# Attention outputs of a fused cross-attention and expert kernel: P V in plain fp32 on two column tiles, softmax sums off TensorE, V kept on chip

## The chip, the cores and the metric

The kernel runs on one core of a Trainium2 chip. The metric is the device time of one execution in microseconds (us). The kernel before was run three times: 1199.52, 1198.44 and 1197.42 us, median 1198.44 us.

## The reference, cut to what matters

```python
# x 2048 x 256, ctx 1601 x 192; 4 heads of 64; keys = 1601 ctx rows (masked) and 2048 latent rows
q = ln @ Wq.T
kv = concatenate([xn @ Wkv.T, ln @ Wlkv.T], axis=1)          # ctx keys, then latent keys
...
qn, kn = rmsnorm(q, qn_g) * SCALE, rmsnorm(k, kn_g)
attn = softmax(where(mask, einsum('bhid,bhjd->bhij', qn, kn), -max), axis=-1)
out = einsum('bhij,bhjd->bhid', attn, v)                     # P V, the part that changes
x = x + out @ Wo.T + bo
...
x = x + top-2 mixture of 8 experts of layernorm(x)           # silu(gate) * up, 256 -> 512 -> 256
```

All arithmetic is fp32, and the kernel keeps close to that precision.

## The kernel before, in words

**Prologue.** The keys make 29 tiles of 128 (NK = 29: 13 of context, 16 of latents). A software pipeline (`pro`, written once for each engine, at lines 440, 575, 757 and 1112) normalises a tile, transposes it, multiplies it by the projection weights in plain fp32 (lines 1129 and 1133), normalises K by head, transposes K, and keeps K on chip as two arrays: S2 with the rounded value (type fp32r), the mask and a row for the maximum; S1 with rounded value and remainder one above the other. V is written to DRAM: ScalarE rounds it (line 593), VectorE forms the remainder (line 786), and SyncE stores both with a column of ones (`v_store`, line 285).

**Attention loop.** A unit is one head and 512 queries, 16 units in all. `v_load` (line 292) brings the V of a head back in two buffers. In a unit the 29 key tiles go in 15 pairs (NP = 15; the last pair has one tile). For a pair p the engines do this:

- TensorE, `scores(p)` (line 1214): for each of the two tiles two fp32r products of 512 columns (lines 1221 and 1222) into one of two score banks bS.
- ScalarE (line 642): the exponential of the pair, 128 x 1024, into PT, which has three slots; then (line 648) the rounded copy Ph.
- VectorE or GpSimd (lines 894 and 482): the remainder Pl = PT - Ph. GpSimd takes six pairs of a unit, VectorE nine.
- TensorE, `outputs(p)` (line 1230), issued two pairs behind the scores: for each tile V rounded times Ph (line 1239, 65 output rows, the 65th being the sum of P by the column of ones), V remainder times Ph (line 1241, 64 output rows) and V rounded times Pl (line 1249), all into the bank bPV.

In between, TensorE computes the row maxima of the next unit in 32 `pieces` of 464 columns (line 1177), in two banks bM; VectorE reduces each (line 867). PE can start piece k only when piece k - 2 was reduced. At the start of a unit the next queries are transposed (`q_T`, line 1162), and ScalarE copies them out in `q_evac` and `q_evac_1` (lines 626 and 629) behind the exponentials of pairs 1 and 2; VectorE forms their remainder (`q_lo`, line 861). At pair 4 the outputs of the unit before are transposed back (`o_T`, line 1191; four transposes at line 1200) and divided by the sums (`o_out`, line 880). At the end the maxima are transposed (`c_T`, line 1180) and put into the queries as a row (line 633), which the next unit's scores wait for; ScalarE copies bPV out (line 652).

Each engine runs its own program in the order written, and waits on semaphores. What sets the order around the change is the list `SLOTS` with the pieces' places, and `POOL_PAIRS`. SyncE and GpSimd meanwhile split the expert weights in 96 chunks (`split`, line 462; `store`, line 323), six in a unit.

**Behind the loop** come the output projection, router and 39 expert blocks, which the change leaves as they are.

Of the kernel before, what the change touches and what calls it, by code (L numbers as in the profile page):

```python
# [17 lines left out]
F32 = mybir.dt.float32  # L18
# [19 lines left out]
VW = 2 * D + 1  # L38
NP = (NK + 1) // 2
NG = -(-KEYS // 512)  # L40
# [49 lines left out]
def build(nc, x, ctx_in, mask, ln_x_g, ln_x_b, ln_l_g, ln_l_b, qn_g, kn_g, w_lat, w_ctx, wo_t, bo,  # L90
          router_t, w13, w2, out):
    xln_d = nc.dram_tensor("xln_d", [TOK, DIM], F32, kind="Internal").ap()
    v_d = nc.dram_tensor("v_d", [H, P, NK, VW], F32, kind="Internal").ap()
# [10 lines left out]
    with stack:  # L104
# [25 lines left out]
        Ph = sb("Ph", [P, 3, 2, QB * P], F32R, at=pro)  # L130
# [13 lines left out]
        top = ExitStack()  # L144

# [9 lines left out]
        st6 = sb("st6", [P, NK, 6], at=t0)  # L155
# [7 lines left out]
        Vs = sb("Vs", [P, 2, H, VW], F32R, at=t0)  # L163
        t0.close()
        t1 = ExitStack()
        V = sb("V", [P, 2, NK, VW], F32R, at=t1)
        Q1 = sb("Q1", [P, 2, QB * P], F32R, at=t1)
        Q2 = sb("Q2", [P, 2, QB * P], F32R, at=t1)
        part = ExitStack()
        PT = sb("PT", [P, 3, 2, QB * P], at=part)  # L170
        part.close()
        Pl = sb("Pl", [P, 3, 2, QB * P], F32R, at=t1)
# [3 lines left out]
        oT_a = sb("oT_a", [P, QB * P], at=t1)  # L176
# [97 lines left out]
        def _(sp):  # L274
# [9 lines left out]

            def v_store(s):
                sp.wait_ge(sem("v_lo"), s.v + 1)
                sp.dma_start(v_d[:, :, s.v, :].rearrange("h p c -> p h c"), Vs[:, s.par, :, :].bitcast(F32))\
                    .then_inc(sem(f"v_st{s.par}"), 16)

            run_steps(sp, 0, NK, v_store)  # L290

            def v_load(h):
                sp.dma_start(V[:, h % 2, :, :].bitcast(F32), v_d[h]).then_inc(sem(f"v_in{h % 2}"), 16)

            for j in range(2):
                sp.wait_ge(sem(f"v_st{j}"), (NK + 1 - j) // 2 * 16)
            sp.wait_ge(sem("klo"), NK)
            sp.wait_ge(sem("s1"), NK)
            sp.wait_ge(sem("q_s"), NT)
            v_load(0)  # L300
            v_load(1)
# [37 lines left out]
            for h in range(H):  # L339
                if h < H - 1:  # L340
                    with sp.Fori(0, EH) as i:
                        expert_split(EH * h + i, False)
                else:
                    for e in range(EH * h, E):
                        expert_split(e, e == E - 1)
                if h + 2 < H:
                    sp.wait_ge(sem("pv"), 3 + NP * NB * (h + 1))
                    v_load(h + 2)
# [65 lines left out]
        def _(pool):  # L414
# [11 lines left out]
            pool.memset(Vs[:, :, :, D:D + 1].bitcast(F32), 1.0).then_inc(sem("v1"), 1)  # L426
# [7 lines left out]
            pool.wait_ge(sem("v1"), 1)  # L434
# [38 lines left out]

            NG_ = len(POOL_PAIRS)
            SHARE = NCH * E // UNITS
            for h in range(H):
                with pool.Fori(0, NB // 2) as i:
                    for j in range(2):
                        u = NB * h + 2 * i + j
                        for n, p in enumerate(POOL_PAIRS):  # L480
                            pool.wait_ge(sem("p_hi"), NP * u + p + 1)
                            pool.tensor_tensor(Pl[:, p % 3, :, :], PT[:, p % 3, :, :],  # L482
                                               Ph[:, p % 3, :, :].bitcast(F32), ALU.subtract)\
                                .then_inc(sem("p_lo_g"), 1)
                            for ch in range(SHARE * n // NG_, SHARE * (n + 1) // NG_):
                                split(E // H * h + i, SHARE * j + ch)

# [67 lines left out]
        def _(act):  # L555
# [19 lines left out]
            def pro(s, b, c):  # L575
# [13 lines left out]
                if b:  # L589
                    act.wait_ge(sem("v_mm"), t.v + 1)  # L590
                    if not (t.i is None and t.off < 2):
                        act.wait_ge(sem(f"v_st{t.par}"), 16 * t.half)
                    act.copy(Vs[:, t.par, :, 0:D], heads(bV[t.par][:, 0, 0:DIM])).then_inc(sem("v_hi"), 1)
# [15 lines left out]
            act.wait_ge(sem("v1"), 1)  # L609
# [24 lines left out]

            def unit(u, j):
                for p in range(NP):
# [4 lines left out]
                    act.wait_ge(sem("pv"), g + 1)  # L641
                    act.activation(PT[:, p % 3, 0:w, :], bS[sl][:, 0:w, :], ACT.Exp).then_inc(sem("exp"), 1)  # L642
# [7 lines left out]
                act.wait_ge(sem("pv"), NP * (u + 1) + 3)  # L650
                act.wait_ge(sem("oT_a"), u + 1)
                act.copy(oT_a[0:D + 1, :], bPV[0:D + 1, 0, :]).then_inc(sem("o_cp"), 1)
# [65 lines left out]
        def _(dve):  # L718
# [38 lines left out]
            def pro(s, a, ln, b, c):  # L757
# [61 lines left out]
            dve.wait_ge(sem("v1"), 1)  # L819
# [69 lines left out]
            def p_lo(u, p):  # L889
                w = 2 if 2 * p + 1 < NK else 1  # L890
                if p in POOL_PAIRS:
                    return
                dve.wait_ge(sem("p_hi"), NP * u + p + 1)
                dve.tensor_tensor(Pl[:, p % 3, 0:w, :], PT[:, p % 3, 0:w, :],  # L894
                                  Ph[:, p % 3, 0:w, :].bitcast(F32), ALU.subtract).then_inc(sem("p_lo"), 1)

            def unit(u, j, last):

                q_stage(u + 1, (u + 1) % UNITS if last else u + 1)
                for p in range(NP):  # L900
                    pieces(u + 1, (p, 0))
                    if p:
                        p_lo(u, p - 1)
                    if p == 2:
                        q_lo(u + 1, (j + 1) % 2)
                    if p == 4:
                        o_out(u)
                    pieces(u + 1, (p, 1))
                    pieces(u + 1, (p, 2))
                    if p == SLOTS[-1][0]:  # L910
                        maxima(u + 1)
                p_lo(u, NP - 1)
# [196 lines left out]
        def _(pe):  # L1109
            pe.wait_ge(sem("ident"), 1)  # L1110

            def pro(s, c, a, b):
# [47 lines left out]
            pe.sem_inc(sem("pv"), 3)  # L1160
# [284 lines left out]
```

## Time and profile before

| | |
|---|---|
| median of three runs | 1198.44 us |
| lowest, highest | 1197.42, 1199.52 us |
| profiled execution | span 1197.7 us from the first to the last instruction |
| prologue | 0 to 139 us |
| first maxima, then 16 units | 139 to 860 us |
| projection, router, experts | 860 to 1198 us |
| mean granted TensorE clock | 0.946 |

The profiled execution has no time recorded for it but its span, which lies between the lowest and the highest run. In the profile PE is TensorE's matmul side, PEld its weight loads (which run beside matmuls), DVE VectorE, ACT ScalarE, POOL GpSimd, SPq and the like the queues of DMA issues. A row of the view in order of time has the start, the duration, the engine, the line, the operation, out<-in and the shapes; an entry in brackets is the idle time before it and who ended it. Matmuls overlap in their tails, so that the distance from one start to the next is what one costs, not its duration. "128*65" is the stationary operand: 128 rows, 65 columns. A fp32r product of 512 columns is one record; a plain fp32 product is two records.

### The profile page before, as it was taken

How to read it: one execution, taken by the hardware profiler on the slowest of the kernel's cores; microseconds unless marked ns; L12 is line 12 of the kernel's file. 1: busy time of each engine (PE TensorE's matmuls, PEld its weight loads, DVE VectorE, ACT ScalarE, POOL GpSimd, SP SyncE). 2: the span in 40 equal slices, each digit the busy share in tenths (PEclk: the TensorE clock that was granted, in tenths of full speed). 3: DMA queues.
4: the chain of work that ended last, by engine and by line, in shares of the span. 5: the costliest groups of instructions: out<-in, count | busy, mean ns of one | idle time of the engine just before them, and what ended most of it. 6: DMA issues, size and time to landing. Idle time of an engine off the chain costs nothing.

```text
span 1197.7 us, 19749 instructions
## 1 busy us (share of the span) xinstructions
PE 1054.0 (88%) x4904; PEld 761.3 (64%) x4905; DVE 774.5 (65%) x1474; ACT 656.9 (55%) x867; POOL 518.0 (43%) x525
## 2 busy tenths in 40 slices
PE   3688689999999999999999999999866268999994
PEld 2455457667666666766666766666555257888884
DVE  4999777766766866766766676686554813444442
ACT  1455446777777777777677677777522012333321
POOL 4012125454544654644645554465410014555553
PEclk9899879999999999999999999999977569999998
DMA  5222402112131111231211211111266777333332
GB/s 162 62 71 71 172 16 69 53 40 70 53 113 58 60 46 53 66 114 45 71 48 48 70 53 49 57 58 47 67 184 209 265 248 199 52 49 52 53 53 26
DMA packets 84392, 100.41 MB, mean 84 GB/s; under 512 B 11035, under 2 KB 78044, under 8 KB 83836
## 3 DMA queue, kind: packets, MB, share of 16 engines
q1 hardware_dynamic: 73694, 89.20, 22.8%
q0 software_dynamic: 7488, 10.23, 5.3%
q10 hardware_dynamic: 3166, 0.46, 0.3%
q8 instruction: 19, 0.31, 0.1%
q14 instruction: 25, 0.20, 0.1%
HBM read 57.60 MB, written 42.26 MB: 83 GB/s over the span
## 4 chain that ended last, share of the span: by engine, by line
PE 70%; DVE 10%; ACT 7%; DMA 5%; issue 5%; SPq 1%; ACTq 1%; DVEq 0%; POOL 0%; POOLq 0%
PE bM L1177 9%; PE bPV L1241 8%; PE bPV L1239 8%; PE bPV L1249 8%; PE bS L1221 7%; PE bS L1222 7%; ACT PT L642 4%; DVE mpart L867 3%; DMA xin<-x 3%; PE bA L1129 2%; PE bG L1340 2%; PE bH L1357 1%; ACT Ph L648 1%; PE bY L1340 1%; PE bY L1342 1%
## 5 line engine op out<-in xcount | busy, mean ns | idle before, releaser
L482 POOL TENSOR_TENSOR Pl<-PT,Ph 128x1024 fp32r<-128x1024 f32 x96 | 230.8, 2404 | 348.5 <-ACT Ph L648 348.5
L867 DVE TENSOR_REDUCE mpart<-bM 128x1 f32<-128x464 f32 x524 | 310.9, 635 | 87.2 <-PE bM L1177 85.9
L642 ACT ACTIVATE PT<-bS 128x1024 f32<-128x1024 f32 (+1 forms) x240 | 239.4, 998 | 139.3 <-PE bS L1222 139.3
L648 ACT CAST Ph<-PT 128x1024 fp32r<-128x1024 f32 (+1 forms) x240 | 245.5, 1023 | 7.0
L894 DVE TENSOR_TENSOR Pl<-PT,Ph 128x1024 fp32r<-128x1024 f32 x144 | 176.1, 1223 | 104.6 <-ACT Ph L648 104.4
L1221 PE MATMUL bS<-Q,S 128*128 128x512 f32 x464 | 185.9, 401 | 1.4 <-ACT Q L633 0.7
L1239 PE MATMUL bPV<-Ph,V 128*65 128x512 f32 x464 | 184.5, 398 | 0.0
L1222 PE MATMUL bS<-Q,S 128*128 128x512 f32 x464 | 184.0, 396 | 0.0
L1241 PE MATMUL bPV<-Ph,V 128*64 128x512 f32 x464 | 183.1, 395 | 0.0
L1177 PE MATMUL bM<-S,Q 128*128 128x464 f32 (+1 forms) x524 | 165.5, 390 | 10.9 <-DVE mpart L867 8.7
L1249 PE MATMUL bPV<-Pl,V 128*65 128x512 f32 x464 | 146.9, 395 | 0.8
L1177 PEld LDWEIGHTS bM<-S,Q 128*128 128x128 f32 x524 | 99.3, 190 | 59.7 <-DVE mpart L867 15.6
L1221 PEld LDWEIGHTS bS<-Q,S 128*128 128x128 f32 x464 | 87.8, 189 | 28.7 <-ACT PT L642 3.7
L1222 PEld LDWEIGHTS bS<-Q,S 128*128 128x128 f32 x464 | 87.9, 189 | 17.7
L470 POOL TENSOR_TENSOR wraw<-wraw,whi 128x256 fp32r<-128x256 f32 x96 | 85.8, 894 | 7.7
L1249 PEld LDWEIGHTS bPV<-Pl,V 128*65 128x65 f32 x464 | 61.7, 135 | 42.5 <-DVE Pl L894 8.2
L1241 PEld LDWEIGHTS bPV<-Ph,V 128*64 128x64 f32 x464 | 62.5, 135 | 38.0
L1239 PEld LDWEIGHTS bPV<-Ph,V 128*65 128x65 f32 x464 | 62.9, 136 | 34.9 <-issue 5.8
L538 POOL DMA_INDIRECT out<-ysb,ring_s x39 | 62.2, 1594 | 41.7 <-POOL ring_s L532 32.3
L1090 DVE TENSOR_TENSOR hs<-hs,bU 128x512 f32<-128x512 f32 x39 | 26.8, 687 | 64.2 <-PE bU L1342 64.2
L710 ACT CAST xTe<-bXe 128x256 fp32r<-128x256 f32 x39 | 14.6, 373 | 88.0 <-PE bXe L1378 88.0
L698 ACT CAST hTe<-bH 128x512 fp32r<-128x512 f32 x39 | 22.9, 587 | 67.8 <-PE bH L1357 67.8
(210 smaller groups left out, 1537.4 us busy)
## 6 DMA issues: line engine op xcount, KB each, us to landing
W<-wsp_d SPq DMA_DIRECT2D x32, 768.0 KB, 5.8
wraw<-w SPq DMA_DIRECT2D x96, 128.0 KB, 2.2
wsp_d<-whi SPq DMA_DIRECT2D x96, 128.0 KB, 1.7
wsp_d<-wraw SPq DMA_DIRECT2D x96, 128.0 KB, 1.7
v_d<-Vs SPq DMA_DIRECT2D x29, 258.0 KB, 3.3
V<-v_d SPq DMA_DIRECT2D x4, 1870.5 KB, 7.6
xall<-x SPq DMA_DIRECT2D x1, 2048.0 KB, 13.6
xin<-x SPq DMA_DIRECT2D x16, 128.0 KB, 3.8
```

What stands on the lines that cost most here:

```text
L470: pool.tensor_tensor(wraw[:, ch % 2, :].bitcast(F32R), wraw[:, ch % 2, :], whi[:, ch % 2, :].bitcast(F32), ALU.subtract).then_inc(sem("wsp ...
L482: pool.tensor_tensor(Pl[:, p % 3, :, :], PT[:, p % 3, :, :], Ph[:, p % 3, :, :].bitcast(F32), ALU.subtract)\
L642: act.activation(PT[:, p % 3, 0:w, :], bS[sl][:, 0:w, :], ACT.Exp).then_inc(sem("exp"), 1)
L648: act.copy(Ph[:, p % 3, 0:w, :], PT[:, p % 3, 0:w, :]).then_inc(sem("p_hi"), 1)
L867: dve.tensor_reduce(mpart[:, i, g:g + 1], banks[k % len(banks)][:, 0:PIECE], AX, ALU.max)\
L894: dve.tensor_tensor(Pl[:, p % 3, 0:w, :], PT[:, p % 3, 0:w, :], Ph[:, p % 3, 0:w, :].bitcast(F32), ALU.subtract).then_inc(sem("p_lo"), 1)
L1177: pe.matmul(banks[k % len(banks)][:, 0:PIECE], Q2[:, par, i * P:(i + 1) * P], S2[:, h, g * PIECE:(g + 1) * PIECE], start=True, stop=True). ...
L1221: pe.matmul(bS[sl][:, b, :], S1[:, h, c * P:(c + 1) * P], Q1[:, j, :], start=True, stop=False)
L1222: last = pe.matmul(bS[sl][:, b, :], S2[:, h, c * P:(c + 1) * P], Q2[:, j, :], start=False, stop=True)
L1239: pe.matmul(bPV[0:D + 1, 0, :], V[:, h % 2, c, 0:D + 1], Ph[:, sl, b, :], start=c == 0, stop=False, skip_group_check=True)
L1241: pe.matmul(bPV[0:D, 0, :], V[:, h % 2, c, D + 1:VW], Ph[:, sl, b, :], start=False, stop=False, skip_group_check=True)
L1249: last = pe.matmul(bPV[0:D + 1, 0, :], V[:, h % 2, c, 0:D + 1], Pl[:, sl, b, :], start=False, stop=c == NK - 1, skip_group_check=True)
```

## The change

V stays in SBUF in fp32 (`V[P, H, NK * D]`); its rounding, remainder, stores and loads go. P is no longer split: PT has four slots and is used in plain fp32. The two tiles of a pair go to two column tiles of the array: tile b of the pair writes output rows 64 b to 64 b + 63 of bPV. The sums of P over the keys leave TensorE: VectorE and GpSimd add up PT in two accumulators (`DVE_SUMS`, `POOL_SUMS`), VectorE merges them at the start of the next unit (`z_merge`), and `o_T` becomes eight plain fp32 products a unit: four that add the two halves by a stacked identity (`twin`) while they transpose, and four with a column of ones (`onec`) that add the sums over the partitions. The pieces are placed by `PIECES`, before and behind the outputs of a pair; they begin at pair 2.

```diff
-        Ph = sb("Ph", [P, 3, 2, QB * P], F32R, at=pro)
+        acc_d = sb("acc_d", [P, 2, QB * P], at=pro)
+        acc_p = sb("acc_p", [P, 2, QB * P], at=pro)
...
-                    act.copy(Vs[:, t.par, :, 0:D], heads(bV[t.par][:, 0, 0:DIM])).then_inc(sem("v_hi"), 1)
+                    act.copy(V[:, :, bass.ds(t.v * D, D)], heads(bV[t.par][:, 0, 0:DIM])).then_inc(sem("v_cp"), 1)
...
-                    dve.wait_ge(sem("v_hi"), t.v + 1)
-                    dve.tensor_tensor(Vs[:, t.par, :, D + 1:VW], heads(bV[t.par][:, 0, 0:DIM]),
-                                      Vs[:, t.par, :, 0:D].bitcast(F32), ALU.subtract).then_inc(sem("v_lo"), 1)
...
+            dve.memset(acc_d[:], 1.0).then_inc(sem("z_d"), len(DVE_SUMS))
+            dve.memset(acc_p[:], 1.0).then_inc(sem("z_p"), len(POOL_SUMS))
...
+            def pt_free(u, p):
+                old = p - NPT if p >= NPT else max(q for q in range(NP) if q % NPT == p)
+                since = 1 if p >= NPT else 0
+                act.wait_ge(sem("pv"), NP * (u + since) + old + 1)
+                for name, sums in (("z_p", POOL_SUMS), ("z_d", DVE_SUMS)):
+                    for n, pair in enumerate(sums):
+                        if old in pair:
+                            act.wait_ge(sem(name), len(sums) * (u + since) + n + 1)
...
-                    act.wait_ge(sem("exp"), g + 3)
-                    act.copy(Ph[:, p % 3, 0:w, :], PT[:, p % 3, 0:w, :]).then_inc(sem("p_hi"), 1)
...
+            def z_merge(v):
+                dve.wait_ge(sem("z_d"), ND * (v + 1))
+                dve.wait_ge(sem("z_p"), len(POOL_SUMS) * (v + 1))
+                dve.tensor_tensor(acc_d[:], acc_d[:], acc_p[:], ALU.add).then_inc(sem("zm"), 1)
+                dve.wait_ge(sem("zm"), v + 1)
+                dve.tensor_tensor(zs[:], acc_d[:, 0, :], acc_d[:, 1, :], ALU.add).then_inc(sem("zs"), 1)
...
             def unit(u, j, last):
                 q_stage(u + 1, (u + 1) % UNITS if last else u + 1)
+                z_merge(u)
+                q_lo(u + 1, (j + 1) % 2)
+                done = 0
+                for k, (before, after) in enumerate(PIECES):
+                    n = sum(sum(x) for x in PIECES[:k])
+                    for m in range(before + after):
+                        piece(u + 1, n + m, M_BANKS)
+                    if n < NM <= n + before + after:
+                        maxima(u + 1)
+                    if k == OUT_AT:
+                        o_out(u)
+                    while done < ND and max(DVE_SUMS[done]) < k:
+                        z_sum(u, done)
+                        done += 1
...
+                pe.wait_ge(sem("zs"), v + 1)
...
-                    last = pe.transpose(bT[:, 0, i * (D + 1):(i + 1) * (D + 1)], oT_a[0:D + 1, i * P:(i + 1) * P],
-                                        ident[0:D + 1, 0:D + 1])
+                    at = i * (D + 1)
+                    pe.matmul(bT[:, 0, at:at + D], oT_a[:, i * P:(i + 1) * P], twin[:], start=True, stop=True)
+                    last = pe.matmul(bT[:, 0, at + D:at + D + 1], zs[:, i * P:(i + 1) * P], onec[:],
+                                     start=True, stop=True)
...
                 def outputs(p):
+                    pe.wait_ge(sem("exp"), NP * u + p + 3)
+                    for b, c in enumerate(range(2 * p, min(2 * p + 2, NK))):
+                        last = pe.matmul(bPV[b * D:(b + 1) * D, 0, :], V[:, h, c * D:(c + 1) * D],
+                                         PT[:, p % NPT, b, :], start=c < 2, stop=c >= NK - 2, skip_group_check=True)
                     last.then_inc(sem("pv"), 1)
...
                 for p in range(NP):
                     scores(p)
                     if p == 0:
                         q_T(u + 1)
-                    pieces((p, 0))
-                    if p == 4:
+                    if p == OUT_AT:
                         o_T(u)
+                    pieces(p, 0)
                     if p >= 2:
                         outputs(p - 2)
-                    pieces((p, 2))
+                    pieces(p, 1)
...
+PIECES = ((0, 0),) * 2 + ((2, 1),) * 8 + ((2, 0),) * 4 + ((0, 0),)
+OUT_AT = 4
+POOL_SUMS = ((0, 1), (-1, 3), (-1, 5), (-1, 6), (-1, 8), (-1, 9), (-1, 11))
+DVE_SUMS = ((2, 4), (-1, 7), (-1, 10), (-1, 12), (-1, 13), (-1, 14))
```

GpSimd's `z_sum` has the form of VectorE's: it waits for the exponential of its pair, adds a slot of PT to acc_p, and its first sum of a unit also waits for the merge. Between its sums it does its six splits, as before.

## Rows read from the trace of the kernel before

**Rows 1.** The page: busy time of the engines over the whole span

```profile
PE 1054.0 (88%) x4904; PEld 761.3 (64%) x4905; DVE 774.5 (65%) x1474; ACT 656.9 (55%) x867; POOL 518.0 (43%) x525
```

**Rows 2.** A stretch of the loop: length; PE, PEld, DVE, ACT, POOL; clock, DMA share, GB/s

```profile
195.00:500.00 305.00, 299.34 (x1327) 204.69 (x1326) 216.76 (x324) 226.53 (x240) 159.49 (x126) 1.00 0.18 61
```

**Rows 3.** Line 652, the copy that ends each unit (min/median/max ns, first, last start)

```profile
L652 ACT COPY oT_a<-bPV x16: 581/582/583, 208.6 to 859.4; 65x512 f32<-65x512 f32 x16
```

**Rows 4.** Groups by line, 144 to 880 us: busy, mean ns, idle before, releaser

```profile
L867 DVE TENSOR_REDUCE mpart<-bM 128x1 f32<-128x464 f32 x524 | 310.9, 635 | 87.2 <-PE bM L1177 85.9
...
L482 POOL TENSOR_TENSOR Pl<-PT,Ph 128x1024 fp32r<-128x1024 f32 x96 | 230.8, 2404 | 348.5 <-ACT Ph L648 348.5
L642 ACT ACTIVATE PT<-bS 128x1024 f32<-128x1024 f32 x224 | 229.9, 1026 | 136.8 <-PE bS L1222 136.8
...
L894 DVE TENSOR_TENSOR Pl<-PT,Ph 128x1024 fp32r<-128x1024 f32 x128 | 160.9, 1257 | 101.6 <-ACT Ph L648 101.5
```

**Rows 5.** TensorE in order of time, inside a unit: start us, us, instruction

```profile
500.29 0.39 PE L1221 MATMUL bS<-Q,S 128*128 128x512 f32 x1
500.52 0.39 PE L1222 MATMUL bS<-Q,S 128*128 128x512 f32 x1
500.74 0.59 PE L1177 MATMUL bM<-S,Q 128*128 x2
501.17 0.39 PE L1239 MATMUL bPV<-Ph,V 128*65 128x512 f32 x1
501.40 0.40 PE L1241 MATMUL bPV<-Ph,V 128*64 128x512 f32 x1
501.63 0.39 PE L1239 MATMUL bPV<-Ph,V 128*65 128x512 f32 x1
```

**Rows 6.** The same view, plain fp32 products of the projections

```profile
102.23 1.96 PE L1129 MATMUL bA<-wl,xT 128*128 128x512 f32 x4 [0.50 <-DVE knat L801]
104.02 1.03 PE L1133 MATMUL bV<-wl,xT 128*128 128x256 f32 x4
...
106.20 1.96 PE L1129 MATMUL bA<-wl,xT 128*128 128x512 f32 x4 [0.50 <-DVE knat L801]
```

**Rows 7.** Weight loads of plain fp32 with 128 columns; then the transposes at line 1200

```profile
906.45 0.63 PEld L1311 LDWEIGHTS bL<-rt,x3T 128*128 128x128 f32 x4
906.92 0.28 PEld L1284 LDWEIGHTS bFT<-ident,ost 128*128 128x128 f32 x2
...
523.12 0.41 PE L1200 MATMUL bT<-ident,oT_a 65*128 65x65 f32 x4
523.33 0.42 PE L1239 MATMUL bPV<-Ph,V 128*65 128x512 f32 x1
```

**Rows 8.** The start of a unit in order of time: start us, us, instruction

```profile
512.83 0.40 PE L1221 MATMUL bS<-Q,S 128*128 128x512 f32 x1
...
513.96 1.03 ACT L642 ACTIVATE PT<-bS 128x1024 f32<-128x1024 f32 x1 [0.35 <-PE bS L1222]
...
515.13 0.41 PE L1221 MATMUL bS<-Q,S 128*128 128x512 f32 x1
...
519.36 0.58 ACT L629 CAST Q<-bT 64x512 fp32r<-64x512 f32 x1
...
520.04 0.68 DVE L861 TENSOR_TENSOR Q<-bT,Q 64x512 fp32r<-64x512 f32 x1 [0.37 <-ACT Q L629]
...
521.32 1.03 PE L1177 MATMUL bM<-S,Q 128*128 128x464 f32 x2 [0.52 <-DVE mpart L867]
```

**Rows 9.** The prologue: all V remainders, then VectorE in order of time

```profile
L786 DVE TENSOR_TENSOR Vs<-bV,Vs 128x256 fp32r<-128x256 f32 x29 | 12.3, 424 | 0.8
...
108.36 0.42 DVE L786 TENSOR_TENSOR Vs<-bV,Vs 128x256 fp32r<-128x256 f32 x1
108.70 0.16 DVE L790 TENSOR_SCALAR rn<-nrm 128x8 f32<-128x8 f32 x1
```

**Rows 10.** VectorE between the prologue and the first unit, in order of time

```profile
139.03 0.91 DVE L850 MEMSET Q<- 64x1024 f32 x1 [0.27 <-issue]
```

More of the change, by code:

```diff
@@ L37 @@
 NB = NT // QB
-VW = 2 * D + 1
 NP = (NK + 1) // 2
+NPT = 4
 NG = -(-KEYS // 512)
@@ L282, in _ @@
             sp.dma_start(wl[:], w_lat.rearrange("(k p) n -> p k n", p=P)).then_inc(sem("wl_in"), 16)
[L285 to L296, printed above, removed]
             sp.wait_ge(sem("klo"), NK)
             sp.wait_ge(sem("s1"), NK)
+            sp.wait_ge(sem("v_cp"), NK)
             sp.wait_ge(sem("q_s"), NT)
-            v_load(0)
-            v_load(1)
             NCH = EW // WC
@@ L471, in split, with z_sum @@
                                    whi[:, ch % 2, :].bitcast(F32), ALU.subtract).then_inc(sem("wsplit"), 1)
-            NG_ = len(POOL_PAIRS)
             SHARE = NCH * E // UNITS
+            NZ = len(POOL_SUMS)
+            def z_sum(u, n):
+                p, q = POOL_SUMS[n]
+                if n == 0:
+                    pool.wait_ge(sem("zm"), u + 1)
+                else:
+                    pool.wait_ge(sem("z_p"), NZ * (u + 1) + n)
+                pool.wait_ge(sem("exp"), NP * u + max(p, q) + 3)
+                one = acc_p[:] if p < 0 else PT[:, p % NPT, :, :]
+                pool.tensor_tensor(acc_p[:], one, PT[:, q % NPT, :, :], ALU.add).then_inc(sem("z_p"), 1)
             for h in range(H):
@@ L479, in _ @@
                         u = NB * h + 2 * i + j
[L480 to L485, printed above, removed]
+                        for n in range(NZ):
+                            z_sum(u, n)
+                            for ch in range(SHARE * n // NZ, SHARE * (n + 1) // NZ):
                                 split(E // H * h + i, SHARE * j + ch)
@@ L640, in unit @@
                     act.wait_ge(sem("s_mm"), g + 1)
-                    act.wait_ge(sem("pv"), g + 1)
-                    act.activation(PT[:, p % 3, 0:w, :], bS[sl][:, 0:w, :], ACT.Exp).then_inc(sem("exp"), 1)
+                    pt_free(u, p)
+                    act.activation(PT[:, p % NPT, 0:w, :], bS[sl][:, 0:w, :], ACT.Exp).then_inc(sem("exp"), 1)
                     if p == 1:
@@ new lines, in z_sum @@
+            def z_sum(u, n):
+                p, q = DVE_SUMS[n]
+                w = 2 if 2 * q + 1 < NK else 1
+                if n:
+                    dve.wait_ge(sem("z_d"), ND * (u + 1) + n)
+                dve.wait_ge(sem("exp"), NP * u + max(p, q) + 3)
+                one = acc_d[:, 0:w, :] if p < 0 else PT[:, p % NPT, 0:w, :]
+                dve.tensor_tensor(acc_d[:, 0:w, :], one, PT[:, q % NPT, 0:w, :], ALU.add).then_inc(sem("z_d"), 1)
+            def z_merge(v):
[4 more added lines that the diff above has]
+                dve.tensor_tensor(zs[:], acc_d[:, 0, :], acc_d[:, 1, :], ALU.add).then_inc(sem("zs"), 1)
@@ L914, in _ @@
+                while done < ND:
+                    z_sum(u, done)
+                    done += 1
             dve.wait_ge(sem("q1w"), 1)
@@ L1408 @@
 LAT_AT = 6
-SLOTS = [(p, c) for p in range(3, NP - 1) for c in ((0, 2) if p % 2 else (1,))][:NM // 2]
-POOL_PAIRS = (2, 4, 6, 8, 10, 12)
-DVE_PAIRS = tuple(p for p in range(NP) if p not in POOL_PAIRS)
-assert len(SLOTS) == NM // 2
+PIECES = ((0, 0),) * 2 + ((2, 1),) * 8 + ((2, 0),) * 4 + ((0, 0),)
+OUT_AT = 4
+POOL_SUMS = ((0, 1), (-1, 3), (-1, 5), (-1, 6), (-1, 8), (-1, 9), (-1, 11))
+DVE_SUMS = ((2, 4), (-1, 7), (-1, 10), (-1, 12), (-1, 13), (-1, 14))
+assert sum(sum(x) for x in PIECES) == NM and len(PIECES) == NP
 FFN_SEGMENTS = ((0, 1, (1, 0, 0)), (1, 2, (1, 1, 0)), (2, NBLK, (1, 1, 1)), (NBLK, NBLK + 1, (0, 1, 1)),
```

98 lines of the change are left out of this document (27 added, 71 removed).

## The prediction, made before the changed kernel was run

> **What bounds the kernel now.** I read the busy times first: TensorE is busy for 88% of the span, VectorE for 65%, no other engine for more [rows 1]. Cut by stretches, the attention loop shows TensorE busy for 299 of 305 us at full clock (1.00, the 2.4 GHz level), VectorE for 217, ScalarE for 227 and GpSimd for 159 [rows 2]. The copy that ends each unit starts at 208.6 us in the first and 859.4 us in the last of 16, so a unit takes 650.8 / 15 = 43.4 us [rows 3]. So inside a unit the order and the cost of TensorE's instructions set the time. The groups say the same from the other side: VectorE waits 85.9 us for pieces from TensorE, ScalarE 136.8 us for scores and GpSimd 348.5 us for P, all waiting down the line from TensorE [rows 4].
>
> In order of time a fp32r product of 512 columns costs 0.23 us from start to start (500.29, 500.52; 501.17, 501.40, 501.63) and two pieces 0.43 [rows 5]. A unit's 58 score products make 13.3 us, its 87 output products 20.0, its 32 pieces 6.9, three sets of transposes about 0.9: 41.1 in all, and 2.3 us of waits.
>
> **P V, the main term.** It loses 87 fp32r products and gains 29 plain fp32 products in two column tiles. Plain fp32 costs what the projections show: four records of 512 columns, that is two products, take 104.02 - 102.23 = 1.79 us, or 0.447 a record and 0.895 a product [rows 6]. No row shows two products in different column tiles at once, so I bound it. From below, both tiles stream side by side the whole time: 0.895 a pair. From above, one after the other: 1.79 a pair. Today's six products cost 1.38. I take a value between them for a reason of order: the two records of one product need the same tile and stand next to each other in the program, and in every row matmuls start in program order. If the order holds over tiles too, the first record of tile B can start only when the second of tile A does. Then a pair is A1, then A2 beside B1, then B2: three steps, 1.34 us. The last two outputs of a unit follow each other directly, and B2 of pair 13 runs beside the first record of pair 14: four steps, 1.79. That makes 13 x 1.34 + 1.79 = 19.2 us against 20.0: **-0.8 us a unit**. The two half-used tiles bring nearly nothing, because the pair is too short a run to overlap.
>
> The Trainium skill (TensorE: Matmul & The Clock Gate, Part 3, on what overlaps) says that matmuls are monotone in start and end also over tiles. The rows agree as far as they go, since none starts out of order; by that rule the sum is the one above.
>
> **o_T.** Four transposes cost 523.33 - 523.12 = 0.21 us of TensorE's time now [rows 7]. They become eight plain fp32 products, 16 records, each with a load of 128 stationary columns and with few moving columns. The nearest row is the router's product: four such loads in 906.92 - 906.45 = 0.47 us, 0.118 each [rows 7]. 16 x 0.118 = 1.9: **+1.7 us a unit**, in line with the pieces and outputs behind it.
>
> **The start of a unit.** With scores(0) at 0 (512.83 in the trace), ScalarE's exponential starts at 1.13 and lasts 1.03, and scores(2) starts at 2.30 when it has ended [rows 8]. Now nothing is asked of the next queries until pair 3; the pieces of pair 3 then wait because VectorE's q_lo stands ahead of their reductions (ScalarE's copy at 519.36, q_lo at 520.04, TensorE held to 521.32) [rows 8]. Over this stretch I count 1.6 us of waits on TensorE. After the change the rounded copies of P are gone, so exp(1) ends at 3.45 and the query copy at 4.02; but the pieces now come at pair 2, before outputs(0), and TensorE reaches them at 3.23: it waits 0.9 us. Exp(2) then runs to 5.05, the second query copy to 5.63, q_lo to 6.4, the first reduction (0.6) to 7.0. TensorE's third piece, behind outputs(0), is reached at 5.89 and waits for that bank to 7.1: 1.2 us more. With 0.1 before scores(2) that makes 2.2 us: **+0.6 us a unit**. The waits for Pl that go are counted in this.
>
> **What lies beside other work.** VectorE drops nine remainders (1.26 us each, one of them short, 11 in all) and gains six sums and two merges (nearest row 1.26, halves 0.7, 9.0 in all) [rows 4]: 2 us a unit less. The merge stands ahead of q_lo and the pieces, but it ends near 3 us, before q_lo's inputs exist. A sum between two pairs' pieces makes VectorE 1.26 us late; a pair of TensorE's work is 0.93 + 1.34 + 0.65 = 2.92 and of VectorE's three reductions 1.9, so it catches up within a pair and costs 0.1 or so. ScalarE drops 15 copies of 1 us and stays far from the bound; its new waits for free slots of PT lie after sums that are at least one pair old. GpSimd goes from six additions of 2.4 us to seven [rows 4]: 159.49 us in 305 is 22.7 a unit, so 25.1 of some 45. Its last sum, of pair 11, is three pairs ahead of the merge that waits for it. Behind that merge stand q_lo, all reductions and through them TensorE; this cover of about 7 us would be gone only if GpSimd's splits were held by DMA. SyncE loses the four loads of V from its queue, which were ahead of nobody on the path.
>
> **Once only.** In the prologue VectorE is the busiest engine, and the V remainder stands in its chain: 108.70 - 108.36 = 0.34 us before the next step can start, 29 times [rows 9]: at most -9.9 us; nothing would be the other end, if another engine took over. I take it whole. Before the first unit VectorE gains two memsets of 1024 columns, 0.91 each by the nearest row [rows 10], and three small ones: +2.2. Behind the last unit nothing covers the merge (about +1.2) and o_T (+1.7). Together **-4.8 us**.
>
> **The sum.** 16 x (-0.8 + 1.7 + 0.6) = +24, less 4.8: +19.2 on the span of 1197.7 us, 1216.9. The median of the runs is 0.7 us above that span: 1217.6, and I say 1218.
>
> **Rival 1, full overlap.** B1 starts beside A1. For it: two 64-column tiles share neither columns nor output rows, and one record takes only half the array. Against it: the order of starts in all rows. P V is 15 x 0.895 = 13.4 us, -6.6 a unit. VectorE then is 2 to 3 us a unit in the way: TensorE's pair takes 2.47 us, so a sum or o_out holds a piece by 0.6 about twice (+1.0), and the wait at the start grows by 1.0. 16 x (-6.6 + 1.7 + 1.0 + 1.0) = -46, with -4.8 it is -51: **1147 us**. It decides if a pair's outputs take under 1.1 us. The Trainium skill's TensorEngine Tiling (Overview, Theoretical Speedup) gives up to 2x for two tiles, which no row here shows; that is this rival.
>
> **Rival 2, no overlap.** The second tile waits until the first is through: 14 x 1.79 + 0.9 = 26.0, +6.0 a unit; 16 x (6.0 + 1.7 + 0.1) - 4.8 = +120: **1319 us**. This is also what comes out if the tiles don't do what they are placed for. For it: no row shows anything run side by side on the array; against it, nothing either.
>
> **Rival 3, a drain at each change of tile shape.** A record lasts 0.40 us but the next starts after 0.23; if the 0.17 of tail had to run out at both ends of each output, that is 30 x 0.17 = 5.1 us a unit, 82 in all: **1300 us**. Against it: the product of 64 output rows now stands between products of 65 in each pair, and costs the same 0.23 as the scores [rows 5], and the program already gives it a tile of half the width. The Trainium skill (TensorEngine Tiling, Key Properties) says that a switch of tiling mode drains TensorE; the rows don't show it, at least for a tile at the same corner.
>
> **How the numbers follow.** Three steps 0.46, full overlap 0.33, no overlap 0.13, drain 0.05, a new wait on GpSimd or a PT slot 0.03 (some tens of us slower). The predicted time is that of the first. Its own range: half a microsecond a unit either way for the waits, and the prologue's gain lost, 1208 to 1236. The range of 8 in 10 takes in rival 1 with its own uncertainty and leaves rivals 2 and 3 out: 1140 to 1240. About 0.2% is what a measurement of this kernel can tell from no change. Faster by more: rival 1 and the far end of the first, 0.37; within: 0.05; slower: 0.58.
>
> **What would show it.** Right: inside a pair, plain fp32 records of P V with starts 0.45 apart, B1 at the start of A2 or a few ns behind, and the next scores 1.34 behind A1; 16 loads of o_T in 1.9 us; a gap near 0.9 before the first piece of a unit and 1.2 before the third; copies of bPV 44.9 us apart. Rival 1 shows B1 starting with A1 or a next score 0.9 behind it, rival 2 a score 1.8 behind, rival 3 gaps of 0.2 where shapes change. The prediction is wrong if the unit is under 43.4 us, or over 46.5 with TensorE waiting for GpSimd or a PT slot. The cycle of a latent tile in the prologue should shrink from 106.20 - 102.23 = 3.97 us [rows 6] by 0.3.

## The result and the profile of the changed kernel

The changed kernel takes 1252.15 us (median of 4 runs, 1244.72 to 1253.06), the kernel before 1197.93 us (4 runs, 1196.78 to 1199.52). The ratio is 1.0435, 95% interval 1.0404 to 1.0465: slower by 52 to 54 us, beyond the predicted range of 1140 to 1240.

The page's busy times, and the copy that ends each unit (min/median/max ns, first and last start), of the changed kernel:

```profile
PE 1053.2 (84%) x4644; PEld 643.9 (51%) x4645; DVE 808.4 (65%) x1436; ACT 415.7 (33%) x627; POOL 569.7 (46%) x540
...
L646 ACT COPY oT_a<-bPV x16: 585/587/590, 209.4 to 911.9; 128x512 f32<-128x512 f32 x16
```

TensorE is busy as long as before but for a smaller share [rows 1]. A unit takes (911.9 - 209.4) / 15 = 46.8 us against 43.4 [rows 3]: 3.4 us more, 51.7 in 15 units. The first copy is 0.8 us later, and what follows the last one takes 339.3 us against 338.3. So nearly all of the 53.5 us between the two spans (1251.2 and 1197.7) lies in the units.

**The outputs.** TensorE in order of time at pairs 5 and 6, with what VectorE and GpSimd do beside it:

```profile
554.40 1.08 PE L1244 MATMUL bPV<-PT,V 128*64 128x512 f32 x4
555.32 2.39 POOL L466 TENSOR_TENSOR acc_p<-acc_p,PT 128x1024 f32<-128x1024 f32 x1 [4.24 <-ACT PT L638]
555.41 0.48 PE L1185 MATMUL bM<-S,Q 128*128 128x464 f32 x1
...
556.49 2.30 DVE L890 TENSOR_TENSOR acc_d<-PT 128x1024 f32<-128x1024 f32 x1
556.64 0.59 PE L1185 MATMUL bM<-S,Q 128*128 128x464 f32 x2
557.16 1.08 PE L1244 MATMUL bPV<-PT,V 128*64 128x512 f32 x4
557.65 1.39 POOL L448 CAST whi<-wraw 128x256 fp32r<-128x256 f32 x1
558.71 1.84 DVE L862 TENSOR_REDUCE mpart<-bM 128x1 f32<-128x464 f32 x3
...
559.39 0.48 PE L1185 MATMUL bM<-S,Q 128*128 128x464 f32 x1 [1.16 <-DVE mpart L862]
```

The four records of a pair's outputs take 555.41 - 554.40 = 1.01 us to the next instruction, not 1.34. How they overlap shows in the busy time of line 1244 in slices of 0.05 us (in parentheses the records that run in a slice: first TensorE, then weight loads):

```profile
551.60:551.65 0.05, 0.02 (x2) 0.02 (x2) 1.00 0.00 0
...
552.05:552.10 0.05, 0.05 (x2) 0.00 (x0) 1.00 0.28 102
552.10:552.15 0.05, 0.05 (x4) 0.00 (x0) 1.00 0.63 225
```

Two records start together at 551.63 and the other two together some 0.47 us later. Both tiles stream side by side from the first record on: that is the overlap of rival 1.

But there is something between them. Two pieces cost 0.43 [rows 5]; from 554.40 back they started at 553.88, so 0.09 went before the outputs, the outputs themselves are 0.11 over 2 x 0.447, and the lone piece behind them takes 0.32 to the next score (555.41, 555.73). An undisturbed pair lasts 2.8 us where the records add up to 2.5.

**VectorE's adds.** In the same rows VectorE's add of pairs 2 and 4 starts at 556.49 and lasts 2.30 us; GpSimd's add had started at 555.32 and ends at 557.71, and 1.08 us later VectorE's is done. GpSimd's cast of a weight chunk starts at 557.65 and lasts 1.39 us, until 0.25 us after VectorE's add. They take turns. The whole trace has 47 adds of VectorE that start during an add of GpSimd, three a unit, and each ends 1.08 or 1.09 us after GpSimd's. The reduction of the piece behind the add comes at 558.71, and TensorE, which needs its bank, is held 1.16 us. The groups by line show how much longer the adds are than the merge, which has the same form but never meets GpSimd:

```profile
L890 DVE TENSOR_TENSOR acc_d<-acc_d,PT 128x1024 f32<-128x1024 f32 x64 | 130.5, 2039 | 2.0
L890 DVE TENSOR_TENSOR acc_d<-PT 128x1024 f32<-128x1024 f32 x16 | 37.1, 2320 | 0.0
L896 DVE TENSOR_TENSOR acc_d<-acc_d,acc_p 128x1024 f32<-128x1024 f32 x17 | 20.8, 1222 | 0.0
```

The wait is inside the duration of the add, not in VectorE's idle time (2.0 us in all). What it does to TensorE shows in TensorE's idle waits over 15 units (us in all, times, longest), first before the change, then after it:

```profile
PE bM L1177 <- DVE mpart L867: 8.5, 15, 0.6
```

```profile
PE bM L1185 <- DVE mpart L862: 54.3, 60, 1.4
PE bM L1185 <- ACT Q L612: 11.8, 15, 1.0
```

Of the 54.3 us for reductions, 16 belong to the start of the unit (1.08 us, 15 times); the other 38 stand behind VectorE's adds.

**The start of a unit**, TensorE in order of time, and then the busy time and the granted clock (the third number from the right) of two stretches:

```profile
539.92 0.40 PE L1234 MATMUL bS<-Q,S 128*128 128x512 f32 x1
541.03 0.69 PE L1185 MATMUL bM<-S,Q 128*128 128x464 f32 x2 [0.72 <-ACT Q L612]
541.64 1.08 PE L1244 MATMUL bPV<-PT,V 128*64 128x512 f32 x4
...
543.81 0.75 PE L1185 MATMUL bM<-S,Q 128*128 128x464 f32 x1 [1.08 <-DVE mpart L862]
544.36 0.63 PE L1233 MATMUL bS<-Q,S 128*128 128x512 f32 x1
...
548.09 0.48 PE L1185 MATMUL bM<-S,Q 128*128 128x464 f32 x1
```

```profile
541.00:544.30 3.30, 2.19 (x7) 0.99 (x8) 1.78 (x3) 1.39 (x2) 1.86 (x1) 0.93 0.00 0
544.30:546.10 1.80, 1.80 (x6) 1.36 (x6) 0.64 (x1) 0.00 (x0) 0.00 (x0) 0.50 0.00 0
```

The two waits are there as forecast: from start to start they cost 541.03 - 539.92 - 0.23 = 0.88 and 543.81 - 541.64 - 1.01 = 1.16 us, for 0.9 and 1.2 (0.72 and 1.08 of it shows as idle time). What I had not forecast follows them: TensorE, busy for 2.19 of 3.3 us, falls to 1.2 GHz, and the scores of pair 3 cost 0.43 us each instead of 0.23. From the held piece to the next lone one it is 4.28 us (543.81 to 548.09), for 2.77 in the undisturbed pair that follows o_T (552.64 to 555.41): some 1.5 us lost. Six of 15 units, this one among them, show the lower clock in the slice at their start; the other nine have the same waits and stay at full clock.

**o_T and the prologue.** The first records of o_T and of the pieces behind it, then TensorE's cycle of a latent tile:

```profile
549.33 0.33 PE L1210 MATMUL bT<-twin,oT_a 128*128 128x64 f32 x2
...
551.03 0.67 PE L1185 MATMUL bM<-S,Q 128*128 128x464 f32 x2
```

```profile
91.11 1.96 PE L1137 MATMUL bA<-wl,xT 128*128 128x512 f32 x4 [0.19 <-DVE knat L791]
...
94.93 1.96 PE L1137 MATMUL bA<-wl,xT 128*128 128x512 f32 x4 [0.35 <-DVE knat L791]
...
98.57 1.96 PE L1137 MATMUL bA<-wl,xT 128*128 128x512 f32 x4 [0.17 <-DVE knat L791]
```

o_T takes 1.70 us, 1.5 more than before [rows 7]. A latent tile takes 3.73 us on average for 3.97 [rows 6]. Between prologue and first unit, in VectorE's order of time:

```profile
133.65 0.06 DVE L837 MEMSET cmax<- 128x4 f32 x1
...
138.17 0.30 DVE L851 COPY qst<-qnat 128x264 f32<-128x264 f32 x1
```

The prologue ends 5.0 us earlier (138.69 before), half of the forecast, and the stretch of memsets is 2.7 us longer.

### The profile page after: what moved, and what is told of

It is laid out like the page before. It is cut to its first block, busy times and chain, and to the rows that moved or that the text cites. A ratio compares the mean times of both kernels' runs of the same rounds, so it can differ in the third digit from the quotient of the medians.

```text
span 1251.2 us, 18895 instructions
## 1 busy us (share of the span) xinstructions
PE 1053.2 (84%) x4644; PEld 643.9 (51%) x4645; DVE 808.4 (65%) x1436; ACT 415.7 (33%) x627; POOL 569.7 (46%) x540
## 4 chain that ended last, share of the span: by engine, by line
PE 58%; DVE 17%; issue 13%; DMA 5%; ACT 3%; DVEq 1%; ACTq 1%; SPq 1%; POOL 0%; POOLq 0%
PE bPV L1244 13%; PE bM L1185 9%; PE bS L1233 7%; DVE mpart L862 6%; PE bS L1234 6%; DVE acc_d L890 3%; DMA xin<-x 2%; PE bA L1137 2%; PE bG L1338 2%; PE bY L1338 1%; PE bY L1340 1%; PE bY L1339 1%; ACT PT L638 1%; PE bT L1210 1%; PE bH L1355 1%
## 5 line engine op out<-in xcount | busy, mean ns | idle before, releaser
L466 POOL TENSOR_TENSOR acc_p<-acc_p,PT 128x1024 f32<-128x1024 f32 x96 | 228.4, 2379 | 173.3 <-ACT PT L638 170.8
L1244 PE MATMUL bPV<-PT,V 128*64 128x512 f32 x928 | 256.2, 619 | 0.0
L1185 PE MATMUL bM<-S,Q 128*128 128x464 f32 (+1 forms) x524 | 192.9, 425 | 72.2 <-DVE mpart L862 58.1
L890 DVE TENSOR_TENSOR acc_d<-acc_d,PT 128x1024 f32<-128x1024 f32 (+1 forms) x80 | 141.6, 1769 | 3.9
L466 POOL TENSOR_TENSOR acc_p<-PT 128x1024 f32<-128x1024 f32 x16 | 37.7, 2358 | 178.2 <-ACT PT L638 178.2
L1244 PEld LDWEIGHTS bPV<-PT,V 128*64 128x64 f32 x928 | 49.2, 136 | 80.0 <-issue 78.9
L448 POOL CAST whi<-wraw 128x256 fp32r<-128x256 f32 x96 | 86.0, 896 | 0.0
L509 POOL COPY ring_g<-gidx 128x1 int32 (+1 forms) x39 | 27.2, 698 | 69.5 <-DVE sidx L1085 61.7
L512 POOL DMA_INDIRECT xg<-xln_d,ring_g x39 | 39.4, 1010 | 32.2 <-POOL ring_g L509 32.2
L1338 PE MATMUL bY<-W,hTe 128*128 x156 | 47.9, 307 | 1.5 <-DVE hTe L1092 1.5
## 6 DMA issues: line engine op xcount, KB each, us to landing
xall<-x SPq DMA_DIRECT2D x1, 2048.0 KB, 13.4
```

What stands on the lines that cost most here:

```text
L448: pool.tensor_copy(whi[:, ch % 2, :], wraw[:, ch % 2, :]).then_inc(sem("whi"), 1)
L466: pool.tensor_tensor(acc_p[:], one, PT[:, q % NPT, :, :], ALU.add).then_inc(sem("z_p"), 1)
L890: dve.tensor_tensor(acc_d[:, 0:w, :], one, PT[:, q % NPT, 0:w, :], ALU.add).then_inc(sem("z_d"), 1)
L1185: pe.matmul(banks[k % len(banks)][:, 0:PIECE], Q2[:, par, i * P:(i + 1) * P], S2[:, h, g * PIECE:(g + 1) * PIECE], start=True, stop=True). ...
L1244: last = pe.matmul(bPV[b * D:(b + 1) * D, 0, :], V[:, h, c * D:(c + 1) * D], PT[:, p % NPT, b, :], start=c < 2, stop=c >= NK - 2, skip_gro ...
L1338: pe.matmul(out_ap, st_hi, w[:, e, 0, lo:lo + n], start=first, stop=False)
```

## The experiments

Theories at this point: A, the start of the unit; B, adds of VectorE and GpSimd that exclude each other; C, the rival to B, that VectorE has too much work whatever GpSimd does; D, that a change of tile width costs TensorE time. Every time is of one run beside runs of the kernel before, unless an interval is given. (1252 is the changed kernel; the spans by which units are compared come from line 646.) The four runs of the changed kernel spread over 8 us, so a few us between single runs say little.

**Pieces from pair 3.**

```diff
-PIECES = ((0, 0),) * 2 + ((2, 1),) * 8 + ((2, 0),) * 4 + ((0, 0),)
+PIECES = ((0, 0),) * 3 + ((2, 1),) * 10 + ((2, 0),) + ((0, 0),)
```

> Only the list of pieces is changed: none at pair 2, three a pair from 3 to 12. Theory A (the unit's start costs: waits of 0.7 us for the next queries and 1.1 us for the first reduction, then some 2.5 us of TensorE at 1.2 GHz, 1.3 us lost): about 2.5 us a unit come back, 16 units, 1251 - 40 = 1211 us, and no stretch of a unit is at 1.2 GHz. Rival B (VectorE and GpSimd adds are what delays the unit): under 10 us come back, since the same pieces wait later.

Measured: 1220.4 us, 32 less. The same stretch of a unit now shows TensorE busy throughout and at full clock:

```profile
519.80:525.00 5.20, 5.20 (x24) 3.16 (x24) 1.70 (x2) 4.04 (x6) 1.35 (x1) 1.00 0.00 0
525.00:528.00 3.00, 3.00 (x14) 1.61 (x13) 2.29 (x4) 1.60 (x2) 2.12 (x2) 1.00 0.00 0
```

In slices of 9 us at the start of each of 15 units the clock is 1.00 in all. A holds, 2 us a unit for the 2.5 expected. TensorE's waits for reductions are still 51.9 us over 15 units: the pieces now wait longer behind VectorE's adds.

**GpSimd's sums of one element.**

```diff
-                pool.tensor_tensor(acc_p[:], one, PT[:, q % NPT, :, :], ALU.add).then_inc(sem("z_p"), 1)
+                pool.tensor_tensor(acc_p[:, 0:1, 0:1], one[:, 0:1, 0:1], PT[:, q % NPT, 0:1, 0:1], ALU.add).then_inc(sem("z_p"), 1)
```

> GpSimd's sums add one element instead of 128 x 1024, so most of the softmax sum is left out. Theory B (an add of VectorE and one of GpSimd exclude each other; VectorE's lasts 2.3 or 3.4 us instead of 1.2 and holds the piece behind it by 1.1 us at pairs 5 and 8 and by about 0.9 at pair 13): VectorE's adds of 128 x 1024 all last about 1.2 us, 3 us a unit come back, 1251 - 48 = 1203 us. Rival C (VectorE simply has too much work): the adds shorten little and the time stays over 1240 us.

Measured: 1202.1 us, 50 less. The adds of line 890 that add to acc_d, five of the six in a unit (min/median/max ns), here and in the changed kernel:

```profile
L890 DVE TENSOR_TENSOR acc_d<-acc_d,PT x80: 692/1225/1261, 189.4 to 856.6; 128x1024 f32<-128x1024 f32 x64, 128x512 f32<-128x512 f32 x16
```

```profile
L890 DVE TENSOR_TENSOR acc_d<-acc_d,PT x80: 691/1226/3408, 191.0 to 910.4; 128x1024 f32<-128x1024 f32 x64, 128x512 f32<-128x512 f32 x16
```

The longest falls from 3.41 to 1.26 us, and the first add of a unit from 2.30 to 1.25 (medians), with VectorE's own work as it was. TensorE's waits for reductions over 15 units fall from 54.3 to 16.1 us, which is what the start of the unit has. B holds, C falls. Some 6 of the 50 us are clock: the lower clock comes in two of 15 units here, for six in the changed kernel.

**VectorE's sums of one element**, the same edit at VectorE's `z_sum`.

> VectorE's six sums of a unit add one element instead of 128 x 1024; that part of the softmax sum is left out. Theory B: the same 3 us a unit, and what VectorE's own 1.2 us per add costs besides, at most 0.1 to 0.3 each: 1190 to 1203 us. Rival C: as VectorE is 7 us a unit lighter, more than in the run with GpSimd's sums thinned by far, below 1180 us.

Measured: 1205.6 us. An add of one element costs 0.16 us alone and up to 2.34 beside GpSimd's:

```profile
L890 DVE TENSOR_TENSOR acc_d<-acc_d,PT x80: 158/160/2343, 190.0 to 858.4; 128x1 f32<-128x1 f32 x80
```

VectorE is busy for 5.8 us a unit less (4.2 less in the run before this one), but the time is no better than there, so C, which expected under 1180 us, falls here too. This run doesn't show that waiting alone costs, though: the same 47 adds still wait for GpSimd, the longest for over 2 us, and TensorE's waits for reductions are the 16.1 us of the run before. Where an add held TensorE it lasted 2.3 or 3.4 us, VectorE's own 1.2 us and the wait together; with either of the two taken away VectorE catches up. The 3.5 us between the two runs are what two more units with the lower clock cost (four of 15, for two).

**Both tiles of a pair in one column tile.**

```diff
-                        last = pe.matmul(bPV[b * D:(b + 1) * D, 0, :], V[:, h, c * D:(c + 1) * D],
+                        last = pe.matmul(bPV[0:D, 0, :], V[:, h, c * D:(c + 1) * D],
```

(with `start` at the first and `stop` at the last tile, and the copy of bPV of 64 rows.)

> Both tiles of a pair go to column tile 0 (the upper half of the output is left out), all else as in the changed kernel. If two column tiles overlap fully in the changed kernel (a pair's outputs in 1.0 us), a pair now takes 1.8 to 1.9 and the unit about 0.9 x 14.5 = 12 us more, less where TensorE waited anyway: 8 to 12, 1251 + 130 to 190 = 1380 to 1440 us. If the overlap were only of the middle third as predicted, 0.45 x 14.5 = 6.5 us more at most, 1355 us or less.

Measured: 1368.4 us, 116 more, or 7.3 a unit. That is between the two expected cases, so the total does not decide; the rows do. The outputs of a pair and the pieces around them:

```profile
633.78 0.58 PE L1185 MATMUL bM<-S,Q 128*128 128x464 f32 x2
634.29 1.93 PE L1244 MATMUL bPV<-PT,V 128*64 128x512 f32 x4
637.17 0.59 PE L1185 MATMUL bM<-S,Q 128*128 128x464 f32 x2
```

At a pair of three pieces I read 1.86 us from the outputs (603.76) to the next piece (605.62), for 1.01 in the changed kernel: one product after the other.

```profile
603.76 1.93 PE L1244 MATMUL bPV<-PT,V 128*64 128x512 f32 x4
605.62 0.48 PE L1185 MATMUL bM<-S,Q 128*128 128x464 f32 x1
```

The 0.85 a pair would be 12 us a unit, 5 more than was measured. TensorE's waits for reductions account for 3.5 of them (54.3 us in 15 units fall to 2.3), and the lower clock, which no unit here shows, for 0.6; the rest is open.

**Both causes out.** The edits of the first two experiments together.

> Both causes taken out at once: pieces from pair 3, and GpSimd's sums of one element (that part of the softmax sum is left out). Alone they gave 1220.4 and 1202.1 against 1252. If they are separate stalls (the wait at the start and TensorE's slow stretch; the adds that exclude each other) they add up: 1252 - 32 - 50 = 1170 us, give or take 5. If one only hides the other, the time stays near 1200.

Measured: 1169.7 us. 32 and 50 add up: two separate stalls. TensorE's waits for reductions are down to 0.6 us in 15 units.

**One column tile, full width.** As the run in one column tile, but with 128 columns (and the copy of bPV of all 128 rows again):

```diff
-                        last = pe.matmul(bPV[0:D, 0, :], V[:, h, c * D:(c + 1) * D],
+                        last = pe.matmul(bPV[:, 0, :], V[:, h, min(c, NK - 2) * D:(min(c, NK - 2) + 2) * D],
```

> As the run with both tiles in column tile 0 (1368 us), but every output product has 128 columns, the V of two key tiles, so that TensorE never changes from 128 x 128 to 128 x 64 tiles and back; the outputs are those of the wrong keys. A pair shows about 0.3 us beyond the sum of its records: 0.09 before the outputs, 0.1 behind them and 0.1 at the next single piece. Theory D (the change of tile width costs this): the gaps go, 14.5 x 16 x 0.2 to 0.3 = 45 to 70 us less, 1300 to 1325 us. Rival: the gaps come with the change from fp32r to plain fp32 or with the lone piece, and stay: 1360 to 1376 us.

Measured: 1309.3 us, 59 less than with 64 columns, for the same records streamed one behind the other. The pair that answers to the one above:

```profile
600.52 0.58 PE L1185 MATMUL bM<-S,Q 128*128 128x464 f32 x2
600.93 1.88 PE L1244 MATMUL bPV<-PT,V 128*128 128x512 f32 x4
...
603.58 0.59 PE L1185 MATMUL bM<-S,Q 128*128 128x464 f32 x2
```

3.06 us from pieces to pieces, for 637.17 - 633.78 = 3.39. D holds: 59 / 16 = 3.7 us a unit, about 0.25 a pair, is the price of going to 64 columns and back. It is measured with both products in one column tile; that two tiles side by side pay the same is taken over, not measured.

**Rebalanced sums.** GpSimd adds pairs 0 to 11, VectorE only the last three, behind its pieces:

```diff
-POOL_SUMS = ((0, 1), (-1, 3), (-1, 5), (-1, 6), (-1, 8), (-1, 9), (-1, 11))
-DVE_SUMS = ((2, 4), (-1, 7), (-1, 10), (-1, 12), (-1, 13), (-1, 14))
+POOL_SUMS = ((0, 1),) + tuple((-1, p) for p in range(2, 12))
+DVE_SUMS = ((12, 13), (-1, 14))
```

with the pieces from pair 3.

> Pieces from pair 3; GpSimd adds pairs 0 to 11 (11 adds), VectorE only 12, 13 and 14, when its pieces are done. Nothing is left out. Theory B: no piece stands behind an add of VectorE any more, so the time comes near that of the run without both causes, about 1170 to 1185 us, faster than the kernel before. Rival: GpSimd, with 11 x 2.4 + 6 x 1.1 = 33 us a unit of some 41, falls behind, and ScalarE waits for slots of PT or VectorE for the merge: 1200 us or more.

Measured: 1157.9 us (4 runs, 1156.7 to 1158.8), ratio to the kernel before 0.9661, interval 0.9644 to 0.9677. Nothing is left out, and it is faster even than the run with both causes out (1169.7), in which VectorE still had its adds between the pieces. A unit takes (816.3 - 204.2) / 15 = 40.8 us:

```profile
L646 ACT COPY oT_a<-bPV x16: 585/586/592, 204.2 to 816.3; 128x512 f32<-128x512 f32 x16
```

TensorE is busy all but throughout (the second number):

```profile
204.20:816.30 612.10, 610.85 (x2580) 318.68 (x2580) 374.93 (x615) 256.86 (x287) 487.74 (x345) 1.00 0.18 58
```

GpSimd does keep ScalarE waiting, 49.9 us in all at line 638, but the exponential has that much room before its outputs: TensorE waits for ScalarE once, 1.2 us, and never for a reduction.

**Double outputs.** The outputs of two pairs behind the scores of each odd pair:

```diff
-                    if p >= 2:
-                        outputs(p - 2)
+                    if p >= 3 and p % 2:
+                        outputs(p - 3)
+                        outputs(p - 2)
...
+                outputs(NP - 3)
-PIECES = ((0, 0),) * 3 + ((2, 1),) * 10 + ((2, 0),) + ((0, 0),)
+PIECES = ((0, 0),) * 3 + ((2, 2), (2, 0)) * 5 + ((2, 0), (0, 0))
```

> As the run with pieces from pair 3 (1220.4 us), but the outputs of two pairs stand together behind the scores of the odd pair, which halves the changes between scores, pieces and outputs. Theory D: 0.2 to 0.3 us seven times a unit come back, 22 to 34 us, less what the pieces lose that now stand closer (0.1 to 0.3 a pair of pairs, up to 30): 1190 to 1215 us. Without a cost of the change: 1220 or more.

Measured: 1219.2 us, no gain over 1220.4 and outside what I expected. Eight records of outputs take 1.87 us, so the changes are halved; but the pieces behind them wait:

```profile
632.21 1.94 PE L1244 MATMUL bPV<-PT,V 128*64 128x512 f32 x8
635.64 1.03 PE L1185 MATMUL bM<-S,Q 128*128 128x464 f32 x2 [1.50 <-DVE mpart L862]
```

VectorE's add there lasts 3.38 us beside one of GpSimd (631.66, and 631.58). This run mixes two effects and doesn't tell them apart. Waits don't explain it alone: TensorE's waits for reductions are 33.9 us in 15 units, less than the 51.9 of the single order. The lower clock, gone there, is back in 4 of 15 units (0.50 from 547.7 to 549.7 us, for one), in the middle of the unit.

**Double outputs with the rebalanced sums.**

> The rebalanced sums (1157.9 us) with the outputs of two pairs together. In the first run with double outputs (1219, no gain over 1220) VectorE's adds still held the pieces, and the new order put four pieces closer together. Theory D with the adds out of the way: half of the 0.33 us of tile changes of a pair comes back, 7 x 16 x 0.33 = 37 us at most, less 0.3 to 0.6 us a pair of pairs that the pieces lose to their two banks (VectorE needs 0.6 for each): 1120 to 1160 us. If it is over 1160, the pieces lose all that the tiles gain, and the double order has no use with two banks.

Measured: 1149.7 us (4 runs, 1148.0 to 1152.8), ratio 0.9589, interval 0.9560 to 0.9619. With the adds out of the way the order is worth 8 us against the single one (the intervals of the two ratios don't meet), a quarter of the 37 that the tile changes alone would give. The pieces in two banks take part of the rest: two pieces that follow closely on two others take 507.67 - 507.05 = 0.62 us instead of 0.43, four times a unit, 12 us in all.

```profile
505.59 0.69 PE L1185 MATMUL bM<-S,Q 128*128 128x464 f32 x2
...
507.05 0.78 PE L1185 MATMUL bM<-S,Q 128*128 128x464 f32 x2
507.67 0.39 PE L1233 MATMUL bS<-Q,S 128*128 128x512 f32 x1
```

Some 17 us stay open. It is the fastest version here.

**Rebalanced sums alone**, pieces from pair 2 as in the changed kernel.

> The changed kernel with the rebalanced sums alone, pieces from pair 2 as in the changed kernel. The start of the unit was worth 32 us, with and without GpSimd's adds. If it is a stall of its own, this gives 1158 + 32 = 1190 us, give or take 6, and a stretch at 1.2 GHz after the waits in each unit; if the rebalanced sums need the pieces to begin at pair 3, over 1200.

Measured: 1194.1 us, 36 over the version with pieces from pair 3. The stall at the start stands by itself. Only three of 15 units now show the lower clock in the slice at their start, such as this one (0.81 over 9 us), so most of the 36 us is the waits and not the clock (27 us of idle time in 15 units: 15.6 for reductions and 11.5 for the queries, for none in the version with pieces from pair 3). The stretch at 1.2 GHz that I expected in each unit isn't there:

```profile
641.40:650.40 9.00, 8.50 (x38) 5.59 (x38) 4.14 (x8) 2.05 (x2) 6.91 (x5) 0.81 0.14 44
```

## Why the prediction was wrong

The sign was right by luck: P V came out 5.8 us a unit cheaper than forecast, and the tile changes and VectorE's adds together some 6 us dearer. The unit takes 46.8 us, over the 46.5 that I named as a sign of being wrong, but TensorE waits there for VectorE's reductions and not for GpSimd or a slot of PT.

- **P V, -0.8 us a unit: wrong.** The step that failed is "if the order holds over tiles too, the first record of tile B can start only when the second of tile A does". The records start two by two, and since those of one tile start 0.45 us apart (1.86 us for four in the run with one column tile), the two that start together are of different tiles; the outputs are 13.4 us of records a unit, as in rival 1, -6.6. The Trainium skill's rule that I leaned on (TensorE: Matmul & The Clock Gate, Part 3), starts in program order over tiles, doesn't hold if the two records of a plain fp32 product stand next to each other; whether they do on the engine, no run here shows. The Trainium skill's up to 2x for two tiles (TensorEngine Tiling, Theoretical Speedup) agrees with 1.01 against 1.86 us a pair.
- **Tile changes, 0: wrong.** I argued from the 64-column products of the kernel before, which cost nothing [rows 5]. In plain fp32 the width costs 3.7 us a unit, some 59 of the 82 us of rival 3. The Trainium skill's rule (TensorEngine Tiling, Key Properties: a change of mode drains) agrees with the two runs in one column tile, and not with [rows 5], if the 64-column products there are in a tile of half the width, as I took them to be; the profile doesn't show it.
- **VectorE's adds, 0.1 each: wrong.** The step is "nearest row 1.26 ... it catches up within a pair". That row is an average over adds that rarely met an addition of GpSimd: one of the nine in a unit. The trace of the kernel before shows the turn-taking, in a stretch from which I had taken other rows:

```profile
521.09 2.39 POOL L482 TENSOR_TENSOR Pl<-PT,Ph 128x1024 fp32r<-128x1024 f32 x1 [10.29 <-ACT Ph L648]
...
523.05 1.51 DVE L894 TENSOR_TENSOR Pl<-PT,Ph 128x1024 fp32r<-128x1024 f32 x1
523.42 1.39 POOL L468 CAST whi<-wraw 128x256 fp32r<-128x256 f32 x1
```

  VectorE's 1.51 us begin while GpSimd's addition runs, and GpSimd's cast, 0.40 us elsewhere, lasts until 0.25 us after VectorE's. In the changed kernel it happens three times a unit, next to pieces, and cost 50 us, of which 6 are clock: 2.7 a unit. Without it the time is inside the range (1202.1 us); so it is with the pieces moved (1220.4). The Trainium skill says it outright (SBUF — State Buffer, Who interferes with whom): a VectorE tensor_tensor with both inputs in SBUF contends with GpSimd's reads, and the later of the two is blocked until the other ends. The trace agrees: VectorE's add ends 1.08 us after GpSimd's, for 1.22 us that it takes alone.
- **The start, +0.6 us a unit: right, but for the clock.** The two waits have the forecast sizes (0.88 and 1.16 us for 0.9 and 1.2). I had not priced the slow clock: 1.5 us in 6 of 15 units, 0.6 a unit. The 2.0 us a unit that moving the pieces gave are no measure of this term: they are against a start without waits, and the kernel before had 1.6 us of waits there.
- **o_T, +1.7 us a unit: right**, 1.5 measured.
- **Once only, -4.8 us:** the prologue gave 5.0 instead of 9.9 and the memsets cost 2.7, so the first unit starts 2.3 us earlier. The step "I take it whole" failed; the tile cycle shrank by 0.24 and not 0.34. The tail cost 1.0, not 2.9.

By the measured terms a unit is -6.6 + 3.7 + 1.5 + 0.6 + 0.6 + 2.7 = +2.5, where 3.4 was measured; 0.9 us stays open. The run with rebalanced sums hints at where it lies: with next to no waits its unit takes 40.8 us, for 41.1 - 6.6 + 1.5 = 36.0 by the records, so the passages between scores, pieces and outputs cost 4.8 us and not only the 3.7 of the tile width. Rival 1 had the overlap right, but with 1.0 us for VectorE's delay where the adds alone cost 2.7, and without the tile changes, it came out 105 us too low.

## What to carry to other kernels

When a change moves work to VectorE and GpSimd at once, don't price it by mean durations: look in order of time at whether the two ran beside each other in the row that the price comes from, since the wait is hidden inside the duration. Put two-input adds in one engine, or where nothing urgent stands behind them; that, together with the start of a unit freed of waits for data that are not yet made, turned +4.4% into -3.4%. And measure narrow tiles where they alternate with full ones, not in a long run of their own.

## What the runs showed of the hardware that was not expected

- Two 64-column tiles fed with plain fp32 stream fully side by side, from the first record: 1.01 us for a pair of 512-column products, 1.86 in one tile.
- Going to 64 columns and back costs about 0.25 us in plain fp32 (1368.4 against 1309.3 us), while 64 and 65 columns in turn in fp32r cost nothing beyond 0.23 us a product [rows 5]. What makes the difference stays open; it wasn't tried.
- A VectorE add that starts during a GpSimd add ends 1.08 us after it, in all 47 cases of the changed kernel; even an add of one element, 0.16 us alone, lasts up to 2.34 us beside one.
- TensorE busy for 2.19 of 3.3 us was followed by 1.2 GHz in 6 of 15 units, and with rebalanced sums in 3 of 15. With the pieces moved it came in none, but for the first run with double outputs, where it came in 4 of 15.
